# Loading x in strips of every fourth partition, 16 quads at a time, and some loads a tile or two later

## Chip, cores and metric

The kernel runs on one core of a Trainium2 chip. The metric is the device time of one execution in microseconds; a smaller time is better.

## The reference

x has 512 samples of 200 fields of 64 numbers, the weight is one 64x64 matrix for each field, all in float32.

```
bilinear = einsum('bie,ied->bid', feature, weight)     # 512 x 200 x 64
out      = einsum('bid,bjd->bij', bilinear, feature)   # 512 x 200 x 200
```

The output is 82 MB, the input 29 MB.

## The kernel before

The 512 samples are cut into 4 groups of 128. A group's samples stand in 32 quads of 2 x 2 samples: two halves (the upper and lower 64 partitions) and two samples of a pair beside each other. x in SBUF is `x_sb`, `[128, 3, 32 quads, 100 fields, 2]`: fields 0 to 99 of a group (part 0) have two buffers, in turn for even and odd groups, and fields 100 to 199 (part 1) have one buffer between them. So part 0 of the next group can be loaded at any time in a group, and part 1 only behind its last readers, the score products of the group's last chunk.

A group is computed in three chunks of 64 fields and a tail of 8. For each chunk, four mix units (the product with the weights, L263) fill `mixed`; ACT and DVE copy them out of PSUM (L345, L347). Then the chunk has 8 tiles. Tile t computes 4 quads in two score units (L292), u = 0 copied out by ACT and u = 1 by DVE (L324) into one of 6 output slots `tile`. The mix units of the next chunk are computed after tiles 1, 3, 5 and 6. The tail is mixed after tile 6 of chunk 0 (L275, L354), and its two units (L309) stand after tiles 2 and 4 of chunk 1.

PE, ACT and DVE walk through the same list of units; a unit has one of four pairs of PSUM banks, so PE can be up to four units ahead of the copies. The copies of tile k wait until slot k mod 6 has been stored.

All data transfers are issued by SP, in one order and on one queue. At the start it issues eight loads of part 0, four of weights, eight of part 1 and two of weights. Then, for each output tile, it waits for both copies and issues two stores of 64 partitions each (every second one, 6,400 bytes per partition; L180), and behind some tiles a load of x: part 0 of the next group behind tiles 0 to 7 of chunk 0 (L152), part 1 of the next group behind tiles 0 to 7 of chunk 2 (L156). A load is 4 quads of all 128 partitions, 3,200 bytes per partition, 400 KB. Part 1 has a semaphore for each load, part 0 one for all eight. `score` waits for load t of part 1 before tile t of chunk 0, and the mix unit that first reads field 100 waits for loads 6 and 7. The first mix unit of a group waits for its whole part 0.

Of the kernel before, what the change touches and what calls it, by code (L numbers as in the profile page):

```python
# [6 lines left out]
GROUPS = 4  # L7
HALVES = 2
QUADS = BATCH // GROUPS // 4
# [3 lines left out]
CHUNK, CHUNKS = 64, 3  # L13
# [2 lines left out]


PART = FIELDS // 2
PIECES = 8
PIECE_QUADS = QUADS // PIECES  # L20
PART0_LOADS = 8

BANK = 512
BANK_PAIRS = 4
# [5 lines left out]
TILES = QUADS // 4  # L30
MIX_AFTER = (1, 3, 5, 6)
TAIL_MIX_AFTER = 6

LAST_WAITED = MIX_AFTER[(PART - CHUNK) // MIX_FIELDS]
TAIL_AFTER = (2, 4)
SLOTS = 6

# [87 lines left out]
def build(nc, x, weight, out, out_tail):  # L125
# [20 lines left out]
    copied = [sem("copied_act"), sem("copied_dve")]  # L146
    slot_out = [sem(f"slot_out{s}") for s in range(SLOTS)]

    def load_part0(eng, g, n):
        size = QUADS // PART0_LOADS  # L150
        quads = slice(n * size, (n + 1) * size)
        eng.dma_start(x_sb[:, 2 * (g % 2), quads], x[g, 0, :, quads]).then_inc(part0_loaded[g % 2], 16)  # L152

    def load_part1(eng, g, p):
        quads = slice(p * PIECE_QUADS, (p + 1) * PIECE_QUADS)
        eng.dma_start(x_sb[:, 1, quads], x[g, 1, :, quads]).then_inc(part1_loaded[p], 16)  # L156

    with nc.Block() as block:

        @block.sync  # L160
        def _(sp):
            def load_w(n):
                own = slice(W_CUTS[n], W_CUTS[n + 1])
                sp.dma_start(w_sb[:, 0, own, :], weight[:, own, :]).then_inc(w_loaded[n], 16)

            for n in range(PART0_LOADS):
                load_part0(sp, 0, n)
            for n in range(MIX_UNITS):
                load_w(n)
            for p in range(PIECES):  # L170
                load_part1(sp, 0, p)
            for n in range(MIX_UNITS, len(W_CUTS) - 1):
                load_w(n)
            for k, (kind, g, *rest) in enumerate(OUT_TILES):
                to = out_tail[g] if kind == "tail" else out[g, rest[0], rest[1]]
                for e in range(2):
                    n = NUMBER[("tail", g, e) if kind == "tail" else ("score", g, *rest, e)]
                    sp.wait_ge(copied[e], COPIES[n][e])
                for i in range(STRIPS):
                    sp.dma_start(to[i::STRIPS], tile[i::STRIPS, k % SLOTS]).then_inc(slot_out[k % SLOTS], 16)  # L180
                if kind == "score" and g + 1 < GROUPS:
                    c, t = rest
                    if c == 0:

                        load_part0(sp, g + 1, t)
                    if c == CHUNKS - 1:

                        load_part1(sp, g + 1, t)
            for s in range(SLOTS):
                sp.wait_ge(slot_out[s], STRIP_STORES * len(range(s, len(OUT_TILES), SLOTS)))  # L190

# [17 lines left out]
        @block.tensor  # L209
        def _(pe):  # L210
            def wait_bank(n, b):


                old = n - BANK_PAIRS
                if old >= 0:
                    for e in READERS[old][b]:
                        if b == 0 or e not in READERS[old][0]:
                            pe.wait_ge(copied[e], COPIES[old][e])

            def wait_copies(n):  # L220
                for e in range(2):
                    pe.wait_ge(copied[e], COPIES[n][e])

            def wait_part0(g):
                pe.wait_ge(part0_loaded[g % 2], 16 * PART0_LOADS * (g // 2 + 1))

            def wait_part1(g, p):
                pe.wait_ge(part1_loaded[p], 16 * (g + 1))

            def w_field(h, field):  # L230
                own, place = own_index(field)
                return w_sb[half_rows(h), 0 if own == h else 1, place, :]

            def x_field(g, h, field):
                part = 1 if field >= PART else 2 * (g % 2)
                return x_sb[half_rows(h), part, :, field % PART, :]

            def x_sample(g, h, quad, pair):
                return x_sb[half_rows(h), g % 2:g % 2 + 2, quad, :, pair]

            def mix(n, g, c, m):
                first = c * CHUNK + m * MIX_FIELDS
                if c == 0 and m == 0:
                    wait_part0(g)
                if g == 0 and c == 0:
                    pe.wait_ge(w_loaded[m], 16)
                    for e in range(2):
                        pe.wait_ge(w_crossed[e], m + 1)
                elif g == 0:

                    pe.wait_ge(w_crossed[2], 2 * ((c - 1) * MIX_UNITS + m + 1 + (c > 1)))
                if first <= PART < first + MIX_FIELDS:

                    for p in range(MIX_AFTER[m] + 1, PIECES):
                        wait_part1(g, p)
                bank = n % BANK_PAIRS * 2
                for r in range(BANK_FIELDS):
                    for swap in range(2):
                        field = first + swap * BANK_FIELDS + r
                        if r == 0:  # L260
                            wait_bank(n, swap)
                        for h in range(HALVES):
                            last = nc.tensor.matmul(  # L263
                                psum[half_rows(h ^ swap), bank + swap, r * HALF_SAMPLES:(r + 1) * HALF_SAMPLES],
                                w_field(h, field), x_field(g, h, field), start=True, stop=True)
                last.then_inc(unit_ready, 1)

            def tail_mix(n, g):
                wait_bank(n, 0)

                if g == 0:
                    pe.wait_ge(w_crossed[2], 2 * (MIX_UNITS + 1))
                for r in range(TAIL):
                    for h in range(HALVES):
                        last = nc.tensor.matmul(  # L275
                            psum[half_rows(h), n % BANK_PAIRS * 2, r * HALF_SAMPLES:(r + 1) * HALF_SAMPLES],
                            w_field(h, TAIL_FIRST + r), x_field(g, h, TAIL_FIRST + r),
                            start=True, stop=True)
                last.then_inc(unit_ready, 1)

            def score(n, g, c, t, u):
                if t == 0 and u == 0:
                    wait_copies(NUMBER["mix", g, c, MIX_UNITS - 1])
                if c == 0 and u == 0 and t <= LAST_WAITED:
                    wait_part1(g, t)
                for a in range(2):
                    quad = 4 * t + 2 * u + a
                    for pair in range(2):
                        for h in range(HALVES):
                            if a == 0 and pair == 0:  # L290
                                wait_bank(n, h)
                            last = nc.tensor.matmul(  # L292
                                psum[half_rows(pair), n % BANK_PAIRS * 2 + h, a * FIELDS:(a + 1) * FIELDS],
                                mixed[half_rows(h), (CHUNKS * g + c) % 2, quad, :, pair],
                                x_sample(g, h, quad, pair), start=True, stop=True)
                last.then_inc(unit_ready, 1)

            def tail(n, g, e):
                if e == 0:
                    pe.wait_ge(zeroed, 1)  # L300
                    wait_copies(NUMBER["tail_mix", g])
                for half_unit in range(2):
                    wait_bank(n, half_unit)
                    for piece in range(2):
                        for pair in range(2):
                            for column in range(4):
                                quad = 16 * e + 8 * half_unit + 4 * piece + column
                                weights = tails[:, quad].rearrange("p b h r -> p (b h r)")
                                last = nc.tensor.matmul(  # L309
                                    psum[column * TAIL_TILE:(column + 1) * TAIL_TILE,  # L310
                                         n % BANK_PAIRS * 2 + half_unit, piece * FIELDS:(piece + 1) * FIELDS],
                                    weights[:, pair * TAIL_TILE:(pair + 1) * TAIL_TILE],
                                    x_sb[:, g % 2:g % 2 + 2, quad, :, pair], start=pair == 0, stop=pair == 1)
                last.then_inc(unit_ready, 1)

            walk(score, tail, mix, tail_mix)
# [89 lines left out]
```

## Time and profile before

| | |
|---|---|
| median of 3 runs | 312.74 us (312.12 to 316.39) |
| profiled execution | 311.45 us, span 309.7 us |
| PE matmul busy | 239.8 us, 77% |
| DVE, ACT busy | 152.7 us (49%), 130.2 us (42%) |
| data queue | 26,080 packets, 111.43 MB, 91.0% of 16 DMA engines |
| read from and written to HBM | 29.49 MB, 81.92 MB |
| mean granted TensorE clock | 0.944 of full speed |

The span is the time from the first to the last recorded instruction or transfer; the execution's own time is 1.75 us longer. A share of the DMA engines is the time that packets took on 16 engines, divided by 16 times the window; since packets overlap a little it can read slightly above 100%.

### The profile page before, as it was taken

What the parts mean: (1) busy time and instruction counts of PE and PEld (TensorE: products, weight loads), DVE (VectorE), ACT (ScalarE), POOL (GpSimd) and SP (SyncE); (2) the same over time, 40 slices, a digit from 0 to 9 for tenths busy, and PEclk for the clock granted to TensorE, in tenths of its full rate; (3) what the DMA queues carried; (4) which work ended last, traced back from release to release, by engine and by line L of the source; (5) the groups of instructions that cost most, each with busy time, mean ns of one, the idle gap of its engine ahead of it and who ended that gap; (6) DMA issues with size and microseconds to landing.
All of it is one profiled execution on the core that took longest, in us unless ns stands there. A gap on an engine that the chain in (4) does not pass through costs nothing.

```text
span 309.7 us, 14622 instructions
## 1 busy us (share of the span) xinstructions
PE 239.8 (77%) x6784; PEld 209.1 (68%) x6784; DVE 152.7 (49%) x180; ACT 130.2 (42%) x181; POOL 12.5 (4%) x23
## 2 busy tenths in 40 slices
PE   0269757999867776899988597989975985999960
PEld 0257746878766665677977496867975975978840
DVE  0253543457654544537756443536653464736650
ACT  1343524346344433345555333344543453544530
POOL 2005700000000000000000000000000000000000
PEclk9996999899999979999999977999998799999995
DMA  7997999859999999968999999997899998577996
GB/s 259 402 421 302 366 395 380 349 218 365 359 400 404 408 414 409 413 245 351 336 415 396 412 418 413 414 392 276 336 354 400 384 418 360 229 310 295 400 410 287
DMA packets 26140, 112.35 MB, mean 363 GB/s; under 512 B 4320, under 2 KB 4320, under 8 KB 25824
## 3 DMA queue, kind: packets, MB, share of 16 engines
q1 hardware_dynamic: 26080, 111.43, 91.0%
q8 instruction: 53, 0.87, 1.0%
q14 instruction: 7, 0.06, 0.0%
HBM read 29.49 MB, written 81.92 MB: 360 GB/s over the span
## 4 chain that ended last, share of the span: by engine, by line
PE 77%; issue 14%; DMA 3%; SPq 1%; DVE 1%; ACT 1%
PE psum L292 50%; PE psum L263 18%; PE psum L309 8%; DMA w_sb<-w_dram 3%; SPq L152 1%; PE psum L275 1%; DVE tile L324 1%; ACT mixed L345 0%; ACT w_sb L359 0%
## 5 line engine op out<-in xcount | busy, mean ns | idle before, releaser
L292 PE MATMUL psum<-x_sb,mixed 64*64 64x200 f32 x3072 | 170.3, 354 | 27.8 <-issue 26.5
L292 PEld LDWEIGHTS psum<-x_sb,mixed 64*64 64x64 f32 x3072 | 134.3, 140 | 47.3 <-issue 35.0
L324 DVE COPY tile<-psum 128x800 f32<-128x800 f32 x100 | 99.2, 992 | 109.7 <-PE psum L292 99.2
L324 ACT COPY tile<-psum 128x800 f32<-128x800 f32 x100 | 82.5, 826 | 86.0 <-PE psum L292 69.4
L263 PE MATMUL psum<-x_sb,w_sb 64*64 64x64 f32 x3072 | 67.9, 230 | 29.9 <-issue 16.2
L263 PEld LDWEIGHTS psum<-x_sb,w_sb 64*64 64x64 f32 x3072 | 66.3, 143 | 31.0 <-issue 29.3
L345 ACT COPY mixed<-psum 64x512 f32<-64x512 f32 x48 | 27.8, 580 | 34.5 <-PE psum L263 33.9
L345 DVE COPY mixed<-psum 64x512 f32<-64x512 f32 x48 | 33.1, 689 | 10.7 <-PE psum L263 9.4
L347 ACT COPY mixed<-psum 128x512 f32<-128x512 f32 x24 | 14.1, 586 | 36.6 <-PE psum L263 36.6
L309 PE MATMUL psum<-x_sb,tails 128*32 128x200 f32 x512 | 25.3, 342 | 1.4 <-issue 1.4
L309 PEld LDWEIGHTS psum<-x_sb,tails 128*32 128x32 f32 x512 | 17.0, 108 | 8.9 <-issue 4.2
L347 DVE COPY mixed<-psum 128x512 f32<-128x512 f32 x24 | 16.6, 691 | 12.4 <-PE psum L263 12.3
L205 POOL COPY w_sb<-w_sb 64x512 f32<-64x512 f32 (+1 forms) x18 | 10.5, 585 | 25.0 <-DMA w_sb<-w_dram 23.4
L359 DVE COPY w_sb<-w_sb 64x512 f32<-64x512 f32 x4 | 1.7, 422 | 13.6 <-DMA w_sb<-w_dram 13.6
L359 ACT COPY w_sb<-w_sb 64x512 f32<-64x512 f32 x4 | 2.5, 617 | 11.0 <-DMA w_sb<-w_dram 10.8
L275 PEld LDWEIGHTS psum<-x_sb,w_sb 64*64 64x64 f32 x128 | 4.3, 133 | 2.2 <-issue 2.2
L275 PE MATMUL psum<-x_sb,w_sb 64*64 64x64 f32 x128 | 4.7, 218 | 0.0
L354 DVE COPY tails<-psum 64x512 f32<-64x512 f32 x4 | 2.8, 695 | 0.9 <-PE psum L275 0.9
L354 ACT COPY tails<-psum 64x512 f32<-64x512 f32 x4 | 2.3, 579 | 0.1
L194 POOL MEMSET tails<- 128x2048 f32 x1 | 1.8, 1804 | 0.3 <-POOLq L387 0.3
L359 ACT ACT_TABLE_LOAD x1 | 1.3, 1283 | 0.7 <-PEq L387 0.7
L387 POOL MEMSET const-float32-0.0<- 128x1 f32 x1 | 0.1, 98 | 0.2 <-issue 0.2
(3 smaller groups left out, 0.3 us busy)
## 6 DMA issues: line engine op xcount, KB each, us to landing
out_dram<-tile SPq DMA_DIRECT2D x192, 400.0 KB, 5.6
x_sb<-x_dram SPq DMA_DIRECT2D x64, 400.0 KB, 7.4
out_tail_dram<-tile SPq DMA_DIRECT2D x8, 400.0 KB, 3.6
w_sb<-w_dram SPq DMA_DIRECT2D x1, 1152.0 KB, 16.7
w_sb<-w_dram SPq DMA_DIRECT2D x4, 256.0 KB, 8.2
w_sb<-w_dram SPq DMA_DIRECT2D x1, 1024.0 KB, 14.5
```

The source lines that it names most:

```text
L152: eng.dma_start(x_sb[:, 2 * (g % 2), quads], x[g, 0, :, quads]).then_inc(part0_loaded[g % 2], 16)
L194: nc.gpsimd.memset(tails[:], 0.0).then_inc(zeroed, 1)
L205: nc.gpsimd.tensor_copy(w_sb[half_rows(h), 1, own, :], w_sb[half_rows(1 - h), 0, own, :]).then_inc(w_crossed[2], 1)
L263: last = nc.tensor.matmul(psum[half_rows(h ^ swap), bank + swap, r * HALF_SAMPLES:(r + 1) * HALF_SAMPLES], w_field(h, field), x_field(g, h ...
L275: last = nc.tensor.matmul(psum[half_rows(h), n % BANK_PAIRS * 2, r * HALF_SAMPLES:(r + 1) * HALF_SAMPLES], w_field(h, TAIL_FIRST + r), x_f ...
L292: last = nc.tensor.matmul(psum[half_rows(pair), n % BANK_PAIRS * 2 + h, a * FIELDS:(a + 1) * FIELDS], mixed[half_rows(h), (CHUNKS * g + c) ...
L309: last = nc.tensor.matmul(psum[column * TAIL_TILE:(column + 1) * TAIL_TILE, n % BANK_PAIRS * 2 + half_unit, piece * FIELDS:(piece + 1) * F ...
L324: copy(tile[:, k % SLOTS, engine], psum[:, bank:bank + 2, 0:2 * FIELDS]).then_inc(copied[engine], 1)
L345: copy(to[half_rows(h)], source[half_rows(1 - h)]).then_inc(copied[engine], 1)
L347: copy(to, source).then_inc(copied[engine], 1)
L354: copy(tails[half_rows(engine), :, 0:4:3, engine, :], source).then_inc(copied[engine], 1)
L359: copy(w_sb[half_rows(engine), 1, own, :], w_sb[half_rows(1 - engine), 0, own, :]).then_inc(w_crossed[engine], 1)
```

## The change

A load of x is now 32 partitions (every fourth, from partition i) and 16 quads: 32 packets of 12,800 bytes where there were 128 of 3,200. There are still eight loads for a part, four strips for quads 0 to 15 and four for quads 16 to 31. Part 1 has two semaphores, one for each 16 quads, which count four loads each. `score` waits before tile 0 for the first and before tile 4 for the second. The waits in `mix` are gone.

`PART0_AFTER` and `PART1_AFTER` say behind which tile each load is issued. Part 0's are counted from chunk 0's tile 0: tiles 1 to 7, and tile 0 of chunk 1. Part 1's are counted from chunk 2's tile 0: tiles 3, 4, 5 and 6 for quads 0 to 15, tile 7 for three strips of quads 16 to 31, and tile 0 of the next group for the last.

```
-PIECES = 8
+PIECES = 2
 PIECE_QUADS = QUADS // PIECES
-PART0_LOADS = 8
+X_STRIPS = 4
+X_LOADS = PIECES * X_STRIPS
+PART1_AFTER = (3, 4, 5, 6, 7, 7, 7, 8)
+PART0_AFTER = (1, 2, 3, 4, 5, 6, 7, 8)
...
+    def x_piece(n):
+        p, i = divmod(n, X_STRIPS)
+        return p, slice(i, None, X_STRIPS), slice(p * PIECE_QUADS, (p + 1) * PIECE_QUADS)
+
     def load_part0(eng, g, n):
-        size = QUADS // PART0_LOADS
-        quads = slice(n * size, (n + 1) * size)
-        eng.dma_start(x_sb[:, 2 * (g % 2), quads], x[g, 0, :, quads]).then_inc(part0_loaded[g % 2], 16)
-
-    def load_part1(eng, g, p):
-        quads = slice(p * PIECE_QUADS, (p + 1) * PIECE_QUADS)
-        eng.dma_start(x_sb[:, 1, quads], x[g, 1, :, quads]).then_inc(part1_loaded[p], 16)
+        p, strip, quads = x_piece(n)
+        eng.dma_start(x_sb[strip, 2 * (g % 2), quads], x[g, 0, strip, quads]).then_inc(part0_loaded[g % 2], 16)
+
+    def load_part1(eng, g, n):
+        p, strip, quads = x_piece(n)
+        eng.dma_start(x_sb[strip, 1, quads], x[g, 1, strip, quads]).then_inc(part1_loaded[p], 16)
...
-                if kind == "score" and g + 1 < GROUPS:
+                if kind == "score":
                     c, t = rest
-                    if c == 0:
-                        load_part0(sp, g + 1, t)
-                    if c == CHUNKS - 1:
-                        load_part1(sp, g + 1, t)
+                    here = TILES * c + t
+                    last, of = (here - TILES * (CHUNKS - 1), g + 1) if c == CHUNKS - 1 else (here + TILES, g)
+                    for n in range(X_LOADS):
+                        if g + 1 < GROUPS and PART0_AFTER[n] == here:
+                            load_part0(sp, g + 1, n)
+                        if 0 < of < GROUPS and PART1_AFTER[n] == last:
+                            load_part1(sp, of, n)
...
             def wait_part1(g, p):
-                pe.wait_ge(part1_loaded[p], 16 * (g + 1))
+                pe.wait_ge(part1_loaded[p], 16 * X_STRIPS * (g + 1))
...
-                if first <= PART < first + MIX_FIELDS:
-                    for p in range(MIX_AFTER[m] + 1, PIECES):
-                        wait_part1(g, p)
...
-                if c == 0 and u == 0 and t <= LAST_WAITED:
-                    wait_part1(g, t)
+                if c == 0 and u == 0 and 4 * t % PIECE_QUADS == 0:
+                    wait_part1(g, 4 * t // PIECE_QUADS)
```

On SP, from the tiles at the end of chunk 2 of the first group to the first tiles of the second group, the program of before issues this (L180 are stores, L156 loads of part 1, L152 loads of part 0):

```order
62 L156 DMA x_sb<-x_dram 128x800
63 L180 DMA out_dram<-tile 64x1600 [waits copied_dve,copied_act]
64 L180 DMA out_dram<-tile 64x1600
65 L156 DMA x_sb<-x_dram 128x800
66 L180 DMA out_dram<-tile 64x1600 [waits copied_dve,copied_act]
67 L180 DMA out_dram<-tile 64x1600
68 L156 DMA x_sb<-x_dram 128x800
69 L180 DMA out_dram<-tile 64x1600 [waits copied_dve,copied_act]
70 L180 DMA out_dram<-tile 64x1600
71 L156 DMA x_sb<-x_dram 128x800
```

The changed program issues there, without the waits shown and with neighbours merged (L191 are stores, L167 part 1, L163 part 0):

```order
28 L191 DMA out_dram<-tile 64x1600 x2
29 L167 DMA x_sb<-x_dram 32x3200
30 L191 DMA out_dram<-tile 64x1600 x2
31 L167 DMA x_sb<-x_dram 32x3200
32 L191 DMA out_dram<-tile 64x1600 x2
33 L167 DMA x_sb<-x_dram 32x3200 x3
34 L191 DMA out_dram<-tile 64x1600 x2
35 L167 DMA x_sb<-x_dram 32x3200
36 L191 DMA out_dram<-tile 64x1600 x2
37 L163 DMA x_sb<-x_dram 32x3200
```

Before, one load followed every tile. Now three follow tile 7 (row 33) and one of part 1 follows tile 0 of the next group (row 35), where part 0's load stood.

On PE, at the first units of the second group, before (L292 is a score product, part1_loaded0 to 5 one load each):

```order
147 L292 MATMUL psum<-x_sb,mixed 64x200 [waits copied_act]
148 L292 MATMUL psum<-x_sb,mixed 64x200 x7
149 L292 MATMUL psum<-x_sb,mixed 64x200 [waits part1_loaded0,copied_dve,copied_act]
150 L292 MATMUL psum<-x_sb,mixed 64x200 x7
...
154 L292 MATMUL psum<-x_sb,mixed 64x200 [waits copied_act,part1_loaded1]
...
160 L292 MATMUL psum<-x_sb,mixed 64x200 [waits copied_dve,part1_loaded2]
```

and in the changed program:

```order
147 L303 MATMUL psum<-x_sb,mixed 64x200 [waits copied_act]
148 L303 MATMUL psum<-x_sb,mixed 64x200 x7
149 L303 MATMUL psum<-x_sb,mixed 64x200 [waits part1_loaded0,copied_dve,copied_act]
150 L303 MATMUL psum<-x_sb,mixed 64x200 x7
...
154 L303 MATMUL psum<-x_sb,mixed 64x200 [waits copied_act]
...
171 L303 MATMUL psum<-x_sb,mixed 64x200 [waits copied_dve,part1_loaded1]
```

The wait at row 149 has the same name and another content: one load issued after tile 0 of chunk 2 before, and four loads issued after tiles 3 to 6 now. The waits between it and tile 4 are gone.

## Rows read from the trace of the kernel before

**Rows 1.** The page: engine busy, data queue (packets, MB, share), DVE's copy.

```profile
PE 239.8 (77%) x6784; PEld 209.1 (68%) x6784; DVE 152.7 (49%) x180; ACT 130.2 (42%) x181; POOL 12.5 (4%) x23
...
q1 hardware_dynamic: 26080, 111.43, 91.0%
...
L324 DVE COPY tile<-psum 128x800 f32<-128x800 f32 x100 | 99.2, 992 | 109.7 <-PE psum L292 99.2
```

**Rows 2.** Windows: length, busy by engine, then granted clock, DMA share, GB/s.

```profile
20.00:25.00 5.00, 2.47 (x55) 1.95 (x59) 1.23 (x2) 1.16 (x2) 0.00 (x0) 0.74 1.03 426
25.00:30.00 5.00, 5.00 (x116) 3.97 (x112) 1.98 (x2) 1.65 (x2) 3.65 (x6) 0.58 0.67 272
75.00:80.00 5.00, 4.81 (x145) 4.02 (x141) 3.24 (x5) 2.54 (x4) 0.00 (x0) 1.00 0.93 370
240.00:245.00 5.00, 5.00 (x72) 5.00 (x70) 1.63 (x2) 1.65 (x2) 0.00 (x0) 0.57 1.01 407
...
78.00:128.00 50.00, 37.30 (x1127) 33.04 (x1118) 26.89 (x32) 21.26 (x30) 0.00 (x0) 0.97 1.02 401
128.00:151.00 23.00, 22.11 (x634) 17.36 (x637) 11.71 (x14) 10.35 (x14) 0.00 (x0) 1.00 0.82 327
151.00:203.00 52.00, 43.48 (x1191) 39.19 (x1184) 27.16 (x33) 22.18 (x31) 0.00 (x0) 0.93 1.01 404
253.00:285.00 32.00, 27.87 (x853) 24.25 (x848) 17.47 (x21) 14.48 (x20) 0.00 (x0) 1.00 0.76 303
```

**Rows 3.** PE's waits in 82:130: us in total, times, longest.

```profile
PE psum L292 <- issue: 11.4, 7, 2.0
PE psum L263 <- issue: 2.1, 2, 1.5
```

**Rows 4.** The chain of waits at the first group's end: start, length, what.

```profile
93.60 3.02 PE psum L292 x55
```

**Rows 5.** The chain in the light stretch 128:151.

```profile
140.11 1.59 PE psum L292 x32
141.70 0.95 PE psum L263 x57
142.65 1.43 PE psum L292 x27
144.08 0.95 PE psum L263 x61
```

**Rows 6.** The data queue in 5:11, 16:23, 24:26 and 301:307, in this order.

```profile
q1 hardware_dynamic: 788, 2.21, 99.9%
...
q1 hardware_dynamic: 886, 2.92, 103.3%
...
q1 hardware_dynamic: 100, 0.85, 101.3%
...
q1 hardware_dynamic: 487, 2.46, 100.1%
```

**Rows 7.** SP's timeline: the loads behind tile 6, first and third boundary.

```profile
95.68 0.71 SPq L156 DMA_DIRECT2D x_sb<-x_dram  x1
...
239.54 1.03 SPq L156 DMA_DIRECT2D x_sb<-x_dram  x1
```

**Rows 8.** Issue to landing: those two loads, and two stores at 63.

```profile
x_sb<-x_dram SPq DMA_DIRECT2D x1, 400.0 KB, 7.2
...
x_sb<-x_dram SPq DMA_DIRECT2D x1, 400.0 KB, 8.2
...
out_dram<-tile SPq DMA_DIRECT2D x2, 400.0 KB, 3.0
```

**Rows 9.** The chain at 23 and at the third boundary.

```profile
23.33 5.61 PE psum L292 x64
...
235.30 3.41 issue
238.71 6.83 PE psum L292 x84
```

**Rows 10.** PE's waits in 241:286.

```profile
PE psum L263 <- issue: 5.1, 4, 2.0
```

More of the change, by code:

```diff
@@ L34 @@
 LAST_WAITED = MIX_AFTER[(PART - CHUNK) // MIX_FIELDS]
+assert LAST_WAITED * 4 >= QUADS - PIECE_QUADS
 TAIL_AFTER = (2, 4)
@@ L164, in load_w @@
                 sp.dma_start(w_sb[:, 0, own, :], weight[:, own, :]).then_inc(w_loaded[n], 16)
-            for n in range(PART0_LOADS):
+            for n in range(X_LOADS):
                 load_part0(sp, 0, n)
@@ L169, in _ @@
                 load_w(n)
-            for p in range(PIECES):
-                load_part1(sp, 0, p)
+            for n in range(X_LOADS):
+                load_part1(sp, 0, n)
             for n in range(MIX_UNITS, len(W_CUTS) - 1):
@@ L180, in _ @@
                     sp.dma_start(to[i::STRIPS], tile[i::STRIPS, k % SLOTS]).then_inc(slot_out[k % SLOTS], 16)
-                if kind == "score" and g + 1 < GROUPS:
+                if kind == "score":
                     c, t = rest
-                    if c == 0:
-                        load_part0(sp, g + 1, t)
-                    if c == CHUNKS - 1:
-                        load_part1(sp, g + 1, t)
+                    here = TILES * c + t
+                    last, of = (here - TILES * (CHUNKS - 1), g + 1) if c == CHUNKS - 1 else (here + TILES, g)
+                    for n in range(X_LOADS):
+                        if g + 1 < GROUPS and PART0_AFTER[n] == here:
+                            load_part0(sp, g + 1, n)
+                        if 0 < of < GROUPS and PART1_AFTER[n] == last:
+                            load_part1(sp, of, n)
             for s in range(SLOTS):
@@ L224, in wait_part0 @@
             def wait_part0(g):
-                pe.wait_ge(part0_loaded[g % 2], 16 * PART0_LOADS * (g // 2 + 1))
+                pe.wait_ge(part0_loaded[g % 2], 16 * X_LOADS * (g // 2 + 1))
             def wait_part1(g, p):
-                pe.wait_ge(part1_loaded[p], 16 * (g + 1))
+                pe.wait_ge(part1_loaded[p], 16 * X_STRIPS * (g + 1))
             def w_field(h, field):
```

## The prediction

> **What bounds the kernel now.** I read the page first [rows 1]: PE is busy 77% of the span, but the data queue alone fills 91.0% of all 16 DMA engines, so the transfers are the first candidate. The windows by stage [rows 2] then show that the kernel alternates. From 78 to 128 us the DMA share is 1.02 and PE is busy 37.3 of 50 us; from 128 to 151 us the share is 0.82 and PE is busy 22.1 of 23 us. The stretch 151:203 reads like the first. The first kind of stretch is chunk 2 of one group and chunk 0 of the next, where each tile sends 800 KB of output and a 400 KB load follows it. I call it the heavy stretch. The second is chunk 1, without loads but with the two tail units; there PE sets the pace (light stretch). In the last group (253:285) the loads of part 0 are missing and the share is 0.76.
>
> The chain of waits agrees. In the heavy stretch PE's work is cut by idle of 1.0 to 2.0 us put down to "issue", 13.5 us of 48 [rows 3]; in the light stretch the chain is PE back to back [rows 5]. What PE waits for there isn't shown. It costs nothing while the DMA engines have work behind them. So time can be saved in the heavy stretches by less DMA work, and in the light ones by a PE that starts earlier or by giving the idle DMA engines something to do.
>
> **Term A, the packets.** The load of 16 quads of 32 partitions carries the same 400 KB as that of 4 quads of 128 partitions, in 32 packets of 12,800 bytes where there were 128 of 3,200. The number of load DMAs stays at 64, so SP issues as many as before. What a packet costs I get from windows with one kind of transfer [rows 6], as engine time per MB (share x window x 16 / MB). Loads of 3,200: at 5:11 it is 0.999 x 6 x 16 / 2.21 = 43.4 us per MB, at 16:23 1.033 x 7 x 16 / 2.92 = 39.6. Stores of 6,400 bytes at 301:307: 1.001 x 6 x 16 / 2.46 = 39.1. The weights, packets of 8,192 and 9,216 bytes, at 24:26: 1.013 x 2 x 16 / 0.85 = 38.1. The x loads are 64 x 0.41 = 26.2 MB. The smallest saving is from the cheapest load row down to the stores: 0.5 x 26.2 / 16 = 0.9 us. The largest is from the dearest load row down to the weights: 5.3 x 26.2 / 16 = 8.7 us. A check on the whole span: 0.910 x 309.7 x 16 = 4,509 us of engine time in all, less 81.92 MB of stores at 39.1, leaves 1,306 us for 29.5 MB of loads, or 44.3 per MB. That is near the dear end, though part of it may be stores that are slower beside loads. I take -5.0 us (-0.9 to -8.7). It counts in full in the heavy stretches, where nothing else is late, and at the start, where PE waits for the x loads and the first weights.
>
> The Trainium skill (DMA: Bandwidth & Descriptors, Why small descriptors are slow) puts a fixed cost of about 3 cycles on each packet of trn2, on a fabric of 850 MHz. An estimate by that page alone: 6,144 packets fewer over 16 engines, 384 each, at 3.5 ns, is 1.4 us. The 4.3 us per MB between the dearest load row and the stores is far more than the page's rule gives, so the row decides.
>
> **Term B, loads that leave the first tiles of chunk 2.** Part 1's loads stood behind tiles 0 to 7 of chunk 2; now they stand behind 3, 4, 5, 6, 7, 7, 7 and tile 0 of the next group. Part 0's go from tiles 0 to 7 of chunk 0 to tiles 1 to 7 and tile 0 of chunk 1. So per group the light stretch gets longer by about two tiles and the same 16 loads stand in 14 tiles. In those tiles PE must keep up with stores alone: three tiles and one mix are 3 x 1.5 + 0.95 = 5.5 us of PE [rows 5], and 2.46 MB of stores at 410 GB/s [rows 6] are 6.0 us. So PE just keeps up. Where it has no lead the share falls to 0.93, as in 75:80 [rows 2]: 0.07 x 6 us x 3 groups = 1.3 us. I take +0.5 (0 to 1.3).
>
> **Term C, the new wait at the group's start.** Before, tile t of chunk 0 waited for quads 4t to 4t+3 alone, a load issued eight tiles earlier. Now the first unit of the group waits for all four strips of quads 0 to 15, and the fourth strip is issued after tile 6 of the chunk before. Take the first boundary. SP issues that tile's load at 95.68 [rows 7] and it lands 7.2 us later [rows 8], at 102.9. PE began tile 0 of the next group at about 93.60 + 3.02 x 32/55 = 95.4, since tile 7 has 32 of those 55 records [rows 4]. So PE will stand still for about 7.5 us, at each of three boundaries. ACT and DVE have no copies then, and SP, after tile 7, waits for tile 0.
>
> That is idle on PE; it costs only what the DMA engines then miss. Behind the awaited strip they still have tile 7's stores and three more loads (the fifth, sixth and seventh, all issued right after tile 7): 0.8 + 1.2 MB, 5.0 us at 410 GB/s. From the landing, PE needs 1.6 us for the tile at full clock, or 2.8 at half (5.61 us for two tiles at 20:30, granted clock 0.58 and 0.74 [rows 2, 9]); the DVE copy takes 0.99 [rows 1]; and a store issued on an empty queue lands 3.0 us later for 1.0 us of data [rows 8], so up to 2.0 us more until data flows. Together 2.6 to 5.8 us against 5.0: a gap of 0 to 0.8. If tile 7's stores have passed before the landing is seen, only the three loads cover it (3.0 us) and the gap is up to 2.8. I take 0.7 at each of the first two. At the second wait, for quads 16 to 31 before tile 4, the last load was issued after tile 0 and has four tiles of time: free.
>
> At the third boundary no part 0 loads follow, so PE sets the pace afterwards and its delay counts. The load is issued at 239.54 [rows 7] and lands 8.2 us later [rows 8], at 247.7; PE began tile 0 at about 240.9 (the 6.83 us row holds the second half of tile 7 first [rows 9]). That is 6.8 us late, but three loads (3.0 us) fewer stand ahead of it, and the 5.1 us of "issue" idle that PE has between 241 and 286 [rows 10] comes with a full queue and should go. So -1.3 to +3.8, take +1.1. Term C is 2 x 0.7 + 1.1 = +2.5 us (-1.3 to +9.4).
>
> **Sum.** -5.0 + 0.5 + 2.5 = -2.0 us. The profiled execution took 311.45 us around its span of 309.7; the median shown is 312.74, 1.3 above, and I take that as scatter. From the median: 310.7 us.
>
> **Rivals.**
> (1) The boundary wait takes more than the packets give: slower. Its place is the first unit of groups 1 to 3. It decides when the queue behind the fourth strip is shorter than PE's restart, that is when the gap is about 3 us three times. Then +9.0, packets -3.0, B +0.5: 319.2. For it: chunk 2's last tiles have only 7 to 8 us of queue [rows 8], and after PE's stop of 3.4 us at 235.3 the granted clock is 0.57 in 240:245 [rows 2, 9]. Against: three loads stand behind tile 7.
> (2) The packets give all that the dear rows say (-8.7) and the wait is covered by those loads: 304.0, or up to 306 with B. For it: the 44.3 per MB of the whole. Against: the load row at 16:23, which is nearly as cheap as stores.
> (3) Nothing to be seen: packets -0.9 and the rest 0 to 1, 312.5. For it: that same row at 16:23.
> (4) A load on 32 partitions runs at half speed, because two engines then write the same part of SBUF at once. A load takes 0.98 us at 417 GB/s; 64 of them doubled are +63 us. Against: the stores go from 64 partitions, every second one, at 410 GB/s [rows 6]. The Trainium skill (DMA: Bandwidth & Descriptors, Rules for kernel authors) asks for 128 partitions for full bandwidth. But SBUF — State Buffer (The DMA port swizzle) gives the port by bits 2 to 4 and 6 of the partition's number, by which every fourth partition still reaches all 16 ports; no row of before shows such a load.
>
> **How the numbers follow.** Forecast 0.50 (307 to 314.5), rival 1 0.14, rival 2 0.20, rival 3 0.13, rival 4 0.03. The predicted time is the forecast's, 310.7. The range goes from rival 2's 304 to rival 1's 319.5 and leaves out about 0.07 on either side. 2%, about what a measurement here can tell from no change, is 6.3 us: faster means below 306.5, which is rival 2 and an edge of the forecast, 0.22; slower means above 319, half of rival 1 and more of its worse end, and rival 4, 0.12; the rest 0.66.
>
> **What would show it.** Term A: in the profile after, some 20,000 packets instead of 26,080 on the data queue, its share times span down by 5 us from 281.8; loads alone at 5:11 below 43 us per MB. Term B: DMA share 0.93 or more in the first three tiles of chunk 2. Term C: PE idle of some 7 us once a group, ended by a DMA of x, with the DMA share staying above 0.85 in that stretch; below 0.6 for 5 us, rival 1 holds. I'd be wrong above all if the granted clock stays low long after these stops, since PE then loses its lead in chunk 0, or if the third boundary costs its full 6.8 us.

## The result, and the profile after

The changed kernel takes 324.25 us (median of 4 runs), the kernel before 313.03 us beside it: a ratio of 1.0348, 95% interval 1.028 to 1.0416. It is slower by 3.5%, outside the range and on the other side of the forecast. The profiled execution has a span of 322.9 us where it was 309.7: 13.2 us more. (A ratio leaves out the executions that are over 1.5% longer than the fastest of the same kernel beside it, a median doesn't; of e4 one execution is then left, so it has no ratio.)

The page after, with the lines that answer to [rows 1]:

```profile
PE 240.0 (74%) x6784; PEld 208.6 (65%) x6784; DVE 152.6 (47%) x180; ACT 130.6 (40%) x181; POOL 12.6 (4%) x23
...
q1 hardware_dynamic: 19936, 111.43, 88.3%
...
L303 PE MATMUL psum<-x_sb,mixed 64*64 64x200 f32 x3072 | 170.4, 359 | 37.6 <-DMA x_sb<-x_dram 22.6
```

PE works as long as before (240 us). The data queue has 6,144 packets fewer, as foreseen. Its engine time is 0.883 x 322.9 = 285.1 us, against 281.8: it rose by 3.3 us where a fall of 5 was forecast. The rest, 9.9 us, is new idle of the DMA engines. The third line has the new wait: 22.6 us of PE's idle before score products ended with a load of x. PE's waits in full (us in total, times, longest):

```profile
PE psum L303 <- DMA x_sb<-x_dram: 22.6, 4, 9.6
PE psum L274 <- issue: 17.8, 11, 3.4
PE psum L274 <- ACT w_sb L370: 14.4, 1, 14.4
PE psum L303 <- issue: 13.6, 13, 3.1
```

The four stops stand in brackets in PE's timeline:

```profile
100.20 5.47 PE L303 MATMUL psum<-x_sb,mixed 64*64 64x200 f32 x64 [5.12 <-DMA x_sb<-x_dram]
176.50 4.90 PE L303 MATMUL psum<-x_sb,mixed 64*64 64x200 f32 x64 [9.60 <-DMA x_sb<-x_dram]
187.36 3.09 PE L303 MATMUL psum<-x_sb,mixed 64*64 64x200 f32 x64 [1.21 <-DMA x_sb<-x_dram]
252.24 4.61 PE L303 MATMUL psum<-x_sb,mixed 64*64 64x200 f32 x64 [6.63 <-DMA x_sb<-x_dram]
```

One stop before tile 0 at each of the three boundaries, of 5.1, 9.6 and 6.6 us, and one of 1.2 us before a tile 4. In exchange PE's "issue" idle fell to 31 us from 43 (26.5 and 16.2 before).

Where in the span the time went is read from a fixed place in each group, the end of the second tail unit. The kernel before has these rows in its chain of waits (start, length, what; the third unit began at 205.62, stopped for 1.38 us and went on):

```profile
64.66 3.00 PE psum L309 x57
...
137.11 3.00 PE psum L309 x59
...
207.47 3.08 PE psum L309 x58
...
277.52 3.00 PE psum L309 x59
```

and the changed kernel these:

```profile
62.46 3.00 PE psum L320 x59
...
139.18 3.00 PE psum L320 x56
...
215.20 3.31 PE psum L320 x61
...
290.76 3.02 PE psum L320 x60
```

With start and length added, a group takes 72.4, 70.4 and 70.0 us before, and 76.7, 76.3 and 75.3 after. So the three groups with a new wait are 4.3, 5.9 and 5.3 us longer, 15.5 in all, everything that the change does in them taken together. The first group is 2.2 us shorter and the stretch behind the last tail unit is 29.1 us in both: 15.5 - 2.2 = 13.3, the whole difference. It doesn't sit in one place but in all three groups that begin with the new wait.

The second boundary in windows of 1 us (length, busy by engine, granted clock, DMA share, GB/s) shows one stop closely:

```profile
174.00:175.00 1.00, 0.00 (x0) 0.00 (x0) 0.00 (x0) 0.00 (x0) 0.00 (x0) 0.50 1.08 454
175.00:176.00 1.00, 0.00 (x0) 0.00 (x0) 0.00 (x0) 0.00 (x0) 0.00 (x0) 0.50 0.96 403
176.00:177.00 1.00, 0.50 (x8) 0.47 (x12) 0.00 (x0) 0.00 (x0) 0.00 (x0) 0.50 1.09 435
177.00:178.00 1.00, 1.00 (x20) 0.81 (x16) 0.00 (x0) 0.00 (x0) 0.00 (x0) 0.50 0.64 260
178.00:179.00 1.00, 1.00 (x20) 0.81 (x16) 0.00 (x0) 0.83 (x1) 0.00 (x0) 0.50 0.12 51
179.00:180.00 1.00, 1.00 (x20) 0.81 (x16) 0.50 (x1) 0.00 (x0) 0.00 (x0) 0.50 0.06 26
180.00:181.00 1.00, 1.00 (x24) 0.85 (x20) 0.49 (x1) 0.24 (x1) 0.00 (x0) 0.76 0.03 13
181.00:182.00 1.00, 1.00 (x65) 0.95 (x60) 0.53 (x1) 0.58 (x1) 0.00 (x0) 1.00 0.30 122
182.00:183.00 1.00, 1.00 (x44) 0.96 (x40) 0.97 (x2) 0.57 (x1) 0.00 (x0) 1.00 1.01 410
```

PE starts again at 176.5 at half clock (0.50, the 1.2 GHz level, after 9.6 us without work). The DMA engines are full until then, nearly idle from 178 to 181, and full again at 182. In 177 to 182 they miss 0.36 + 0.88 + 0.94 + 0.97 + 0.70 = 3.9 us. The chain of waits through the same place names the steps:

```profile
167.94 8.22 DMA x_sb<-x_dram
...
176.50 2.98 PE psum L303 x32
...
179.50 1.00 DVE tile L335
...
180.58 0.50 SPq L191
...
181.97 5.34 DMA x_sb<-x_dram
```

The awaited load is issued at 167.94 and lands 8.2 us later, at 176.16; one tile of score products takes 2.98 us, DVE's copy 1.0, and SP issues its stores at 180.58. The last row is a load's flight and not a stop: the load behind tile 0 is issued at 181.97 and lands at 187.3, and PE works until 186.1, so that it stands before tile 4 for 1.2 us.

### The profile page after: what moved, and what is told of

Its sections match the earlier page's. It is cut to its first block, busy times and chain, and to the rows that moved or that the text cites. A ratio compares the mean times of both kernels' runs of the same rounds, so it can differ in the third digit from the quotient of the medians.

```text
span 322.9 us, 14602 instructions
## 1 busy us (share of the span) xinstructions
PE 240.0 (74%) x6784; PEld 208.6 (65%) x6784; DVE 152.6 (47%) x180; ACT 130.6 (40%) x181; POOL 12.6 (4%) x23
## 4 chain that ended last, share of the span: by engine, by line
PE 69%; DMA 11%; issue 10%; SPq 5%; ACT 1%; DVE 1%
PE psum L303 45%; PE psum L274 15%; DMA x_sb<-x_dram 8%; PE psum L320 8%; SPq L191 2%; DMA w_sb<-w_dram 2%; SPq L163 2%; PE psum L286 1%; SPq L167 1%; DVE tile L335 1%; ACT mixed L356 1%; ACT tile L335 0%; ACT w_sb L370 0%; ACT mixed L358 0%; SPq L189 0%
## 5 line engine op out<-in xcount | busy, mean ns | idle before, releaser
L303 PE MATMUL psum<-x_sb,mixed 64*64 64x200 f32 x3072 | 170.4, 359 | 37.6 <-DMA x_sb<-x_dram 22.6
L274 PE MATMUL psum<-x_sb,w_sb 64*64 64x64 f32 x3072 | 64.7, 227 | 32.3 <-issue 17.8
L274 PEld LDWEIGHTS psum<-x_sb,w_sb 64*64 64x64 f32 x3072 | 63.5, 141 | 35.4 <-issue 33.6
L220 POOL COPY w_sb<-w_sb 64x512 f32<-64x512 f32 (+1 forms) x18 | 10.6, 588 | 25.0 <-DMA w_sb<-w_dram 23.4
L286 PE MATMUL psum<-x_sb,w_sb 64*64 64x64 f32 x128 | 5.0, 218 | 0.9 <-issue 0.9
L286 PEld LDWEIGHTS psum<-x_sb,w_sb 64*64 64x64 f32 x128 | 4.5, 133 | 1.0 <-issue 1.0
```

Source lines behind the costliest of these rows:

```text
L220: nc.gpsimd.tensor_copy(w_sb[half_rows(h), 1, own, :], w_sb[half_rows(1 - h), 0, own, :]).then_inc(w_crossed[2], 1)
L274: last = nc.tensor.matmul(psum[half_rows(h ^ swap), bank + swap, r * HALF_SAMPLES:(r + 1) * HALF_SAMPLES], w_field(h, field), x_field(g, h ...
L286: last = nc.tensor.matmul(psum[half_rows(h), n % BANK_PAIRS * 2, r * HALF_SAMPLES:(r + 1) * HALF_SAMPLES], w_field(h, TAIL_FIRST + r), x_f ...
L303: last = nc.tensor.matmul(psum[half_rows(pair), n % BANK_PAIRS * 2 + h, a * FIELDS:(a + 1) * FIELDS], mixed[half_rows(h), (CHUNKS * g + c) ...
```

## The experiments

Two theories were set up. **Theory W:** the wait before tile 0 for a load issued late stops PE, and the DMA engines run dry before the next stores come. **Theory P:** loads of 12,800-byte packets from 32 partitions are themselves dearer. All results are medians, with the ratio to the kernel before measured beside each.

| run | what differs | us | ratio (95%) |
|---|---|---|---|
| changed kernel | | 324.25 | 1.035 (1.028 to 1.042) |
| e1 | part 0 in strips, places as before | 315.54 | 1.012 (1.001 to 1.023) |
| e2 | part 0 in blocks of 32 partitions | 329.12 | 1.055 (1.043 to 1.068) |
| e3 | changed, without strips | 326.40 | 1.048 (1.036 to 1.059) |
| e4 | changed places only | 313.58 | median before 313.27 |
| e5 | two strips, 8 quads | 315.06 | 1.011 (1.003 to 1.020) |
| e6 | changed, strips issued early | 315.66 | 1.007 (1.002 to 1.012) |
| e7 | before, and the wait | 327.81 | 1.054 (1.046 to 1.062) |
| e8 | changed, last load a tile earlier | 323.45 | 1.036 (1.027 to 1.045) |
| e9 | before, and the wait in group 1 | 317.77 | 1.026 (1.014 to 1.038) |
| e10 | before, and the wait in group 3 | 318.74 | 1.029 (1.016 to 1.041) |
| e11 | part 0 in two loads of 128 partitions | 315.23 | 1.020 (1.012 to 1.027) |
| e12 | loads of 8 quads, 128 partitions | 317.98 | 1.026 (1.016 to 1.037) |

### e1 and e2: strips and blocks for part 0

e1, in the kernel before:

```
-        size = QUADS // PART0_LOADS
-        quads = slice(n * size, (n + 1) * size)
...
+        p, i = divmod(n, 4)
+        strip = slice(i, None, 4)        # e2: slice(32 * i, 32 * (i + 1))
+        quads = slice(p * 16, (p + 1) * 16)
...
```

> The kernel of before, but part 0 is loaded in strips of every fourth partition, 16 quads each (packets of 12,800 bytes), behind the same tiles as before. Part 1 and all waits stay. Theory W (the new wait before tile 0 stops PE, and the DMA engines run dry behind it: all of the loss): no such wait here, so 311 to 314 us, as before. Theory P (the loads of 12,800-byte packets from 32 partitions themselves cost more engine time, 564 ns a packet in the changed kernel where its median is 479): half of the loads are changed, so half of the loss or more, 316 to 319 us, and the engine time of the data queue rises by about 1.6 us over the 281.8 of before.

> As the strips of part 0 alone, but a load takes 32 neighbouring partitions (0 to 31, 32 to 63, ...) and not every fourth. Theory W: 311 to 314 us. Theory P, in the form that engines meet at the same part of SBUF: neighbouring partitions meet more often, so slower than the strips, 320 us or more, and the first eight loads land well after 12.8 us.

e1 is 1.2% slower, with an interval from 0.1 to 2.3%. Its 315.54 us lie between the ranges expected of the two theories, so e1 alone doesn't decide; e3 and e6 below do. Its data queue reads

```profile
q1 hardware_dynamic: 23008, 111.43, 90.1%
```

which is 0.901 x 313.9 = 282.8 us of engine time against 281.8, so the packets that were saved gave nothing back. e2 is 5.5% slower. The cause is seen in the window 5:11, where nothing but x loads runs (columns as above). In e1:

```profile
5.00:11.00 6.00, 0.00 (x0) 0.00 (x0) 0.00 (x0) 0.00 (x0) 0.00 (x0) 1.00 0.94 374
```

and in e2:

```profile
5.00:11.00 6.00, 0.00 (x0) 0.00 (x0) 0.00 (x0) 0.00 (x0) 0.00 (x0) 1.00 1.01 222
```

With the same packets, neighbouring partitions load at 222 GB/s with the engines busy all the time, and every fourth partition at 374. That is the fourth rival's mechanism, and it strikes the block and not the strip. It agrees with the rule of the Trainium skill (SBUF — State Buffer, The DMA port swizzle) that bits 2 to 4 and 6 of the partition's number choose the port: 32 neighbours differ in bits 2 to 4 alone and reach half of the ports.

### e3 and e4: the places and the wait without the strips

e3 is the changed kernel with the old loads; e4 is the kernel before with the two tables of places.

```
...
-        p, strip, quads = x_piece(n)
-        eng.dma_start(x_sb[strip, 1, quads], x[g, 1, strip, quads]).then_inc(part1_loaded[p], 16)
+        quads = slice(4 * n, 4 * (n + 1))
+        eng.dma_start(x_sb[:, 1, quads], x[g, 1, :, quads]).then_inc(part1_loaded[n // X_STRIPS], 16)
```

> The changed kernel, but a load is again 4 quads of all 128 partitions; places and waits are the changed ones (PE waits before tile 0 for four loads, the last issued after tile 6). Theory W: nearly all of the loss stays, 320 to 325 us, and PE waits some 20 us for x in three places. Theory P: most of the loss is gone, 313 to 317 us.

> The kernel of before with the changed places of the loads alone (part 0 behind tiles 1 to 8, part 1 behind 3, 4, 5, 6, 7, 7, 7, 8); a load is 4 quads of 128 partitions and each tile waits for its own, as before. Tile 0 needs a load issued after tile 3, five tiles earlier. Both theories: 312 to 315 us. Above 317 would say that the later places alone cost time, through the longer stretch without loads.

This decides between the theories. e3 has no strips and the whole loss, 1.048; PE's waits show the same 22.6 us (before tile 0 it stops for 7.3, 6.6 and 6.2 us):

```profile
PE psum L303 <- DMA x_sb<-x_dram: 22.6, 5, 7.3
```

e4 issues the loads at the same late places, but each tile waits for its own: 313.58 beside 313.27, with its four executions between 306.7 and 314.4. So neither the late places nor the longer stretch without loads cost anything that can be measured, as long as no tile must wait for a load that has only just been issued. Between e3 and the changed kernel the strips seem rather to help than to harm (324.3 against 322.9 in the spans, data queue 0.884 x 324.3 = 286.7 against 285.1), within what such runs scatter.

### e5 and e6: strips without the late wait

e5 sets `PIECES = 4`, `X_STRIPS = 2` and part 1's places to 1 to 8, and keeps the mix unit's wait for the last piece. e6 is

```
-PART1_AFTER = (3, 4, 5, 6, 7, 7, 7, 8)
+PART1_AFTER = (3, 3, 3, 3, 7, 7, 7, 7)
```

> The changed kernel with two strips of every second partition and 8 quads in place of four and 16: packets of 6,400 bytes, eight loads a part, four semaphores for part 1, its loads behind tiles 1 to 7 of chunk 2 and tile 0. Tile 0 then needs a load issued after tile 2, four tiles earlier than the changed kernel's. Theory W (the late strip is the loss): 311 to 316 us, and no wait of PE for x. Rival P2 (loads in strips cost more beside stores, as the 553 ns a packet of the strips of part 0 show, and the gain of fewer packets is eaten): 315 to 318 us, with the data queue's engine time at 282 us or above.

> The changed kernel with part 1's loads behind tiles 3, 3, 3, 3 and 7, 7, 7, 7: strips, packets and waits are the changed ones, but the last strip that tile 0 waits for is issued three tiles earlier, and the last one of the other half one tile earlier. Theory W: most of the loss goes, 312 to 317 us; PE waits for x under 5 us in all, where it waited 22.6. If the loss were in the strips and packets, it stays at 322 or more.

e6 differs from the changed kernel in nothing but the places of four loads, with the same strips, packets and semaphores, and recovers four fifths of the loss (1.007 for 1.035). PE's wait for x is 7.6 us where it was 22.6:

```profile
PE psum L303 <- DMA x_sb<-x_dram: 7.6, 4, 3.5
```

Before tile 0, where the changed kernel stops for 5.1, 9.6 and 6.6 us, it has one stop of 0.3 us for x. The others, 2.2, 3.5 and 1.6 us, are before tile 4, and the DMA engines stay full behind the longest of them, which ends at 180.65:

```profile
179.00:186.00 7.00, 5.35 (x113) 4.94 (x117) 1.44 (x2) 1.65 (x2) 0.00 (x0) 0.76 1.02 419
```

So stops of up to 3.5 us before tile 4, with stores and loads of part 0 queued meanwhile, are nearly free here. I had expected under 5 us of waiting. e5 has no wait of PE for x and comes out at 315.06, which lies in both ranges that were expected of it, and its data queue has 0.901 x 314.2 = 283.1 us of engine time, on the side of rival P2. It shows that strips without the late wait lose little, and doesn't say whether that little is the strips' own. Neither kernel is faster than the kernel before.

### e7 to e10: the wait by itself

e7 changes nothing but what PE waits for (e9 and e10 keep the old waits and add one for loads 1 to 6 before tile 0 of group 1 or 3 alone):

```
-                    for p in range(MIX_AFTER[m] + 1, PIECES):
+                    for p in range(7, PIECES):
...
-                if c == 0 and u == 0 and t <= LAST_WAITED:
-                    wait_part1(g, t)
+                if c == 0 and u == 0 and t == 0:
+                    for p in range(7):
+                        wait_part1(g, p)
```

> The kernel of before, loads and places as before, with one change: PE waits before tile 0 of a group for loads 0 to 6 of part 1, where it waited for load 0 (and the mix waits for load 7). Nothing is transferred later or otherwise. Theory W: the stop of PE alone costs as much as the changed kernel or more, 322 to 335 us, since only one load and the stores of tile 7 stand behind the awaited load, not three; PE waits for x about 7 us in each of three groups, and the DMA share falls below 0.6 for 5 us behind each. If the places of the loads mattered more than the stop, 313 to 318.

> The changed kernel with the last load of part 1 behind tile 7 (3, 4, 5, 6, 7, 7, 7, 7), not behind tile 0 of the next group. The stop before tile 0 stays; the second stop, before tile 4 (5.3 us at 182 in the changed kernel's trace, and two of that kind in the trace with the places and waits alone), should go. Theory W with the first stop as the main cost: 320 to 324 us, within 3 of the changed kernel. If the second stop carries much of it: 316 to 319.

> The kernel of before with the wait for loads 0 to 6 before tile 0 in the second group only (first boundary). The wait in all groups cost 15 us (ratio 1.0537). If each boundary costs alike: 4 to 6 us, ratio 1.013 to 1.019. As the prediction had it (0.7 us with a cover of three loads, up to 3 without): at most 1.01. If the loss stood only at the last boundary, where no loads follow and PE sets the pace: 1.00.

> The same in the last group only (third boundary). Alike at each boundary: ratio 1.013 to 1.019. If the last one carries most of it: 1.03 or more.

e7 transfers everything as before, in the same order behind the same tiles, and costs 5.4%. Its three boundaries, in windows of 15 us:

```profile
95.00:110.00 15.00, 9.06 (x190) 7.82 (x186) 4.34 (x6) 4.29 (x7) 0.00 (x0) 0.72 0.73 286
172.00:187.00 15.00, 7.66 (x156) 6.66 (x160) 2.83 (x4) 2.40 (x4) 0.00 (x0) 0.56 0.69 268
255.00:270.00 15.00, 9.06 (x237) 8.24 (x241) 5.35 (x6) 3.89 (x5) 0.00 (x0) 0.71 0.68 272
```

The DMA engines miss 0.27 to 0.32 of 15 us, 4.1, 4.7 and 4.8 us, where the heavy stretch had 1.02 and 1.01 [rows 2]. e8 takes the second stop away (PE's waits for x are three, 21.2 us in all) and stays at 1.036. Its expectation calls that stop 5.3 us, which was the load's flight; the stop was 1.2 us. So e8 shows only that such a short stop is worth nothing measurable, and that four loads behind the awaited one, where the changed kernel has three, save nothing either. e7 has one load and tile 7's stores there; its interval lies above the changed kernel's, though it overlaps that of e3, which has three loads. So more cover helps somewhat at most. e9 and e10 have one wait each and cost 2.6 and 2.9%, both more than the 1.3 to 1.9 expected, though the lower ends of the intervals, 1.4 and 1.6, allow it. In this comparison the kernel before read from 307.3 to 316.9 us, with a median of 314.7, and against that median e9 and e10 are 1.0 and 1.3% slower; so the size is uncertain by 1 to 2%. The profiles say the same from tail unit to tail unit: the group with the wait takes 76.8 us in e9 and 77.0 in e10, where the same groups took 72.4 and 70.0 before. But e9's next group, which has no wait, takes 73.5 for 70.4, so a single group scatters by some 3 us. A wait costs time at either boundary, and no difference between them is shown.

### e11 and e12: larger packets without strips

```
-PART0_LOADS = 8
+PART0_LOADS = 2
...
-                        load_part0(sp, g + 1, t)
+                        if t % 4 == 0:
+                            load_part0(sp, g + 1, t // 4)
```

e12 does the same with loads of 8 quads for both parts.

> The kernel of before, but part 0 comes in two loads of 16 quads over all 128 partitions, behind tiles 0 and 4 of chunk 0: the packets of 12,800 bytes without the strips. If the packet's size is a gain that the strips lose again: the packets' mean is near their median of 479 ns (the strips of part 0 had 553), the data queue's engine time falls by some 2 us below 281.8, and the time is 310 to 313 us. If larger packets suffer beside stores whatever their partitions: a mean above 530 ns and 313 to 316 us.

> The kernel of before with loads of 8 quads over all 128 partitions (packets of 6,400 bytes, 800 KB a load), part 0 behind tiles 0, 2, 4, 6 and part 1 behind tiles 1, 3, 5, 7 of chunk 2, each awaited by the first tile that reads it, seven tiles later. Half of the packets' gain for both parts and no stop: 310 to 313 us if packets are worth anything, 313 to 315 if not.

e11's engine time is 0.898 x 313.5 = 281.5 us, as before: packets of 12,800 bytes save nothing even when they go to all 128 partitions. By the ratios the kernel is 2.0% slower, which I hadn't expected, and e12 is 2.6% slower; against the median of 314.7 of the kernel before they are 0.2 and 1.0% slower, so how much they lose is open. None of the five kernels with larger packets and no long stop (e1, e5, e6, e11, e12) is faster than the kernel before. In e11 PE's idle put down to "issue" is 51 us where the kernel before has 43:

```profile
PE psum L293 <- issue: 28.1, 15, 3.6
PE psum L264 <- issue: 23.2, 15, 3.5
```

e1, with loads of 400 KB, has 47 us (24.0 and 23.4), so the 1.6 MB in one piece can't be the whole reason. That these stops make e11 slower was not tested.

## Why the prediction was wrong

**What bounds the kernel: right.** Heavy stretches filled by the DMA engines, light ones by PE. That a stop of PE is free while the engines have work was right too, as nearly as can be measured; e6, with 7.6 us of stops and 0.7% of loss, shows it.

**Term C, the failed step:** "Behind the awaited strip they still have tile 7's stores and three more loads (the fifth, sixth and seventh, all issued right after tile 7): 0.8 + 1.2 MB, 5.0 us at 410 GB/s." The forecast gave +2.5 us for three boundaries, and their groups are 15.5 longer. The stops were sized well on the whole: 7.5, 7.5 and 6.8 us foreseen, 5.1, 9.6 and 6.6 measured. The restart was sized well too, at its long end: the awaited load lands at 99.95, 176.16 and 251.99, SP issues the next stores 4.3 to 4.4 us later, and at the second boundary the share rises again only in 181:182, so that some 5.5 us pass, where I had 2.6 to 5.8. One tile took 2.98 us there, because the granted clock was 0.50.

What failed is the cover. From the landing at 176.16 the shares of the windows leave 0.84 x 1.09 + 0.64 + 0.12 + 0.06 + 0.03 = 1.8 us of work for the mean engine, not 5.0. A share of 0.06 is one engine of sixteen: from 179 on only one still worked. SP's timeline has the three covering loads as one piece, the last of them issued 0.6 us before its end, at 173.0:

```profile
171.00 2.59 SPq L167 DMA_DIRECT2D x_sb<-x_dram  x3
```

and the time from issue to landing of that last one is

```profile
x_sb<-x_dram SPq DMA_DIRECT2D x1, 400.0 KB, 7.9
```

It landed at 180.9, 4.7 us after the awaited one. So the slowest engine did have the cover that I had counted, and the other fifteen had less. The shares of 0.06 and 0.03 up to the landing show it: a load has landed when the slowest of the 16 has done its share, and the others are by then further on in the same queue, most of them here by some 3 us. I took the queue behind the load as if all engines stood at the same place, though the landing is by its nature seen at the one that is furthest behind.

At the other two boundaries the engines ran dry closer together:

```profile
102.00:103.00 1.00, 1.00 (x20) 0.80 (x16) 0.00 (x0) 0.69 (x1) 0.00 (x0) 0.50 0.80 333
103.00:104.00 1.00, 1.00 (x20) 0.80 (x16) 0.80 (x1) 0.00 (x0) 0.00 (x0) 0.50 0.78 324
104.00:105.00 1.00, 1.00 (x20) 0.80 (x16) 0.19 (x1) 0.47 (x1) 0.00 (x0) 0.50 0.19 77
...
254.00:255.00 1.00, 1.00 (x20) 0.80 (x16) 0.00 (x0) 0.73 (x1) 0.00 (x0) 0.50 0.94 384
255.00:256.00 1.00, 1.00 (x24) 0.84 (x20) 0.76 (x1) 0.00 (x0) 0.00 (x0) 0.71 0.43 170
256.00:257.00 1.00, 1.00 (x44) 0.94 (x40) 0.31 (x2) 0.80 (x1) 0.00 (x0) 1.00 0.03 13
```

With the full windows before them the cover was 3.9 and 3.6 us. Against a restart of 5.5 us the three gaps are 1.6, 3.7 and 1.9 us, 7.2 in all, where I had put 0.7 at each of the first two. That is about half of the 15.5 us. The other half isn't traced to single steps.

In the second group the missed 3.9 us aren't all of the 5.9. The windows of the whole group (second tail unit to second tail unit) read, before and after:

```profile
140.10:210.60 70.50, 60.53 (x1703) 52.67 (x1704) 37.66 (x45) 31.60 (x44) 0.00 (x0) 0.95 0.98 392
```

```profile
142.20:218.50 76.30, 58.57 (x1700) 48.93 (x1700) 37.70 (x44) 31.73 (x44) 0.00 (x0) 0.93 0.92 358
```

The engines miss 1.4 us before and 6.1 after, 4.7 more, and work 69.1 and 70.2 us, 1.1 more (each to about 0.4 us, by the rounding of the shares). In the same way the first group misses 1.8 us more and works 2.5 more, and the third misses 3.8 more and works 1.6 more. No run separates what the half clock of the first tile adds to a stop.

At the third boundary a second step failed. I had PE's delay made good by "the 5.1 us of "issue" idle", which "should go". It stayed; PE's waits in 252:303 of the changed kernel have 3.0 + 1.0 + 0.9 + 0.5 = 5.4 us of it:

```profile
PE psum L274 <- issue: 3.0, 2, 2.2
PE psum L320 <- issue: 1.0, 1, 1.0
PE psum L286 <- issue: 0.9, 1, 0.9
PE psum L303 <- issue: 0.5, 1, 0.5
```

**The first rival** held in its direction. It asked for a gap of about 3 us three times; the gaps were 1.6, 3.7 and 1.9, and the groups lost 5 us each. (Its own sum gives 319.2, the range ends at 319.5.) Its chance of 0.14 was too small, since the gap of "0 to 0.8" holds for the slowest engine and not for the others. **The third boundary** was thought special, since PE sets the pace behind it. By the tail rows it costs 5.3 us against 4.3 and 5.9, and e9 and e10 show no difference between the places. **The second wait**, before tile 4, was called free because four tiles lie between. PE did stop there once, for 1.2 us before 187.36, since the load behind tile 0 is issued later by the length of the first stop while PE then goes on without a pause; e8 shows that this costs nothing measurable.

**Term A, -5.0 forecast, +3.3 measured.** The price of packets was real where loads run alone. The changed kernel's data queue in 5:11 has 0.927 x 6 x 16 / 2.26 = 39.4 us per MB

```profile
q1 hardware_dynamic: 257, 2.26, 92.7%
```

against 43.4 [rows 6]. But it wasn't to be had beside stores: e1, with half of the loads changed, has 1.0 us more engine time than before, and e11 0.3 less. I had applied a difference between windows of loads alone to loads among stores, and the check on the whole span (44.3 per MB) put down to the packets what it could not tell from other causes. The packets in the two traces settle it: over the whole span a load's packet took 137.5 ns on the mean for 3,200 bytes before and 564.1 ns for 12,800 bytes in the changed kernel, which is 43.0 and 44.1 us per MB, no gain at all. The Trainium skill's 3 cycles a packet (DMA: Bandwidth & Descriptors, Why small descriptors are slow), by the prediction's estimate 1.4 us of saving, would have been much nearer.

The rise of 3.3 us splits in two: 2,048 x 564.1 less 8,192 x 137.5 ns, over 16 engines, is 1.8 us for the loads, and 12,800 store packets at 253.3 ns for 251.3 are 1.6 us. Neither the stops nor the strips alone explain it. e7, with the packets of before and long stops, has 0.868 x 328.5 = 285.1 us, the same as the changed kernel; but e8, with strips and long stops, has 0.881 x 321.3 = 283.1, and e6, with strips and short stops, 0.913 x 310.8 = 283.8. Its cause stays open.

**Term B, +0.5.** In 80:90, about the middle of chunk 2 (its first load of x is issued at 84.90), the share fell from 1.00 to 0.86 in the changed kernel, below the 0.93 forecast, 1.4 us in this group. e4, which has the same places, shows no loss that can be measured, so this seems to be given back later.

**"What PE waits for there isn't shown"**, the prediction says of the "issue" idle. The trace of the kernel before does show it, by its timing; the last point of this document has it.

**Rivals 2 and 3** fell. **Rival 4** was false for strips of every fourth partition and true for blocks (e2).

## What to carry to other kernels

Ask of each new wait how long before it its last transfer is issued, and against that hold the time that the queue takes: here 6.7 to 8.2 us from issue to landing, about three tiles. Moving the issue three tiles ahead gave back four fifths of the loss with everything else the same. Don't count the transfers that are queued behind an awaited one in full as cover for the restart: it is seen to land when the slowest DMA engine has done its share, and the others may by then have used up part or most of what lies behind (here 1.8 to 3.9 us were left of 5.0). A price per packet read where only loads run need not hold where loads and stores mix.

## What the runs showed of the hardware that I had not expected

- A load into 32 neighbouring partitions runs at 222 GB/s and one into every fourth partition at 374, with the same packets.
- Packets of 12,800 bytes lower the engine time per MB from 43.4 to 39.4 us when loads run alone (the window 5:11), and not over the whole span, where most loads run beside stores (43.0 and 44.1 us per MB).
- In a full queue the 16 DMA engines don't stand at the same place: after the last issue before a restart the share falls from full to nearly nothing over 1 to 3 us, with 0.64, 0.12, 0.06 and 0.03 from 177 on, 0.78 and 0.19 from 103 on, and 0.43 and 0.03 from 255 on.
- PE's idle put down to "issue" is 43 us before, 31 us in the changed kernel and 51 us in e11. It stands in stretches where the DMA engines are full and hardly in those where they are not [rows 3, 5]. The page has 53 transfers of 0.87 MB on the instruction queue, and PE has 2 x 6,784 = 13,568 instructions, 256 for each of 53. The Trainium skill (Runtime: NRT & Kernel Launch, Instruction fetch mechanics) says that an engine's instructions are refilled in blocks of 16 KiB, 256 of them, mostly hidden. The trace of the kernel before bears out the blocks: if its matmul and weight load records are counted together in order, 29 stops of over 0.3 us, 43.7 us in all, lie in front of records whose numbers differ by multiples of 256, and PE goes on 1.2 to 1.6 us after the end of an instruction transfer each time. In the light stretch the next transfer starts 0.3 us behind such a mark (at 135.04 and 139.21), and from 85 to 127 us, with full DMA engines, 2.9 to 3.8 us behind it. So by their timing the stops are refills that come late when the DMA engines are full, and here they are not hidden. No run changed them on purpose.
